# Second attention's scores: one step on four quarters of TensorE's array, instead of two steps on its column halves

## The chip, the cores and the metric

One core of one Trainium2 chip. The metric is the device time of one execution in microseconds (us), lower is better. The kernel before takes 833.54 us, median of 3 runs (831.65 to 834.04).

## The reference

The input is 16 sequences of 512 rows of 128 numbers, f32. Cut to what matters:

```python
x = layernorm(x + attn(x))       # 16 heads of 8, softcap 50 by tanh, causal softmax over 512 rows
x = layernorm(x + ffn(x))        # below, for each of the 16 sequences

weights = x @ router_w + router_b            # a router picks the 63 best rows of 512
sel_idx = sort(top_k(weights, 64).indices[:63])
hn = rmsnorm(x[sel_idx], ln1)
q, kk, v = rope(heads(hn @ wq)), rope(heads(hn @ wk)), heads(hn @ wv)   # 16 heads of 8
sc = einsum('bhqd,bhkd->bhqk', q, kk) / sqrt(8) + m_sel                 # 63 x 63 for each head
a = softmax(sc)
x1 = x[sel_idx] + (a @ v) @ wo
x2 = x1 + gelu(rmsnorm(x1, ln2) @ w1) @ w2
out = zeros.at[sel_idx].set(x2 * weights[sel_idx]) + x * (1 - sel_mask)
```

The change is in `sc`, the scores of this second attention, over the selected rows.

## The kernel before, in words

**Units of work.** The first attention goes batch by batch (16), the routed part goes pair by pair (8 pairs of batches, "q" in the code): the 64 slots of one batch of a pair lie on partitions 0 to 63, those of the other on 64 to 127. The work is cut into steps in six tracks: `prep` (transposes, the query/key and value projections of a batch), `fin` (end of the first attention: divide, output projection, layernorm), `route`, `sel` (gather the selected rows, project them, rotate), `att` (second attention and the first half of the MLP) and `late`. The core of the first attention stands outside the tracks: TensorE's `scores` (L1182, five banks, two units for each group of two heads), ScalarE's tanh (L716) and exp (L731), GpSimd's causal mask (L627), TensorE's `pv` (L1199).

**The order.** An iteration `p` has 16 slots with two halves each. In every half TensorE issues one scores unit and then what `PE_ORDER` lists for that half; ScalarE, GpSimd and VectorE go through their own loops with `ACT_ORDER`, `POOL_ORDER` and `VE_ORDER`. All is written out by hand in these tables, each engine runs its list strictly in order, and waits on semaphores that count the steps of a track. "att.S0@-2" in iteration p is the step for pair p-2, "prep.qk0/1@0" is for the second batch of pair p. GpSimd widens the keys (`att_kw`) in the slot before its last mask of a pair.

**Banks.** Besides the five banks of scores and the one of `pv`, all steps share two PSUM banks, "a" (`ps_a`) and "m" (`ps_m`). `BANK` says which one a step writes, and `BANK_READ` which readers on VectorE TensorE waits for before it writes there.

**The steps of this text.** The keys of a pair (`qkT[:, 1]`, 128 rows of head x 8 + d, 64 slots of each batch) are widened by GpSimd to `k_wide`: for each batch 16 copies, one per head, each multiplied by a mask `head_of` that leaves only that head's 8 rows (L629, called from `att_kw`, two products of 128x1024). A product of the queries (128 rows x 64 slots) with 8 of the 16 copies (512 columns) then gives the scores of 8 heads on 64 partitions, those of one batch. So S0 (`att_scores(q, 0)`, L1356, bank m) is two such products for heads 0 to 7, batch 0 on the left 64 columns of the array and batch 1 on the right; S1 is the same for heads 8 to 15, into bank m again, and waits until VectorE has read S0. Each product in f32 leaves two records in the trace. VectorE reads with `sc` (L1036, scale and add the mask `msel`), then `mx` (L1042, maximum) and `pm` (L1043, subtract), first for S0 and then for S1, with `sc` and `mx` in the same buffers both times. ScalarE's exp of `pm` (L698) follows, and the transposes P0, P1 of the probabilities, copied into `PT` (L1055), which lies in `k_wide`'s memory.

Around them on TensorE: `prep.qk0/1` (L1230, here "qk0"), half of the query/key projection of a batch, bank a; `pv.4/1` and `pv.5/1` (L1199), which start the second half of a batch's heads and wait for GpSimd's masks; `route.thr/1` (L1281), one transpose. On VectorE: `msel` (L1028), and `fin.y0/1` (L877, L879, `y_tm`), which reads bank a. On GpSimd: the masks (two rows of L627 for each group of two heads), and `z_base` (L629).

## Time and profile before

| | |
|---|---|
| Time, median of 3 runs | 833.54 us (831.65 to 834.04) |
| The profiled execution: span from its first to its last instruction | 830.0 us |
| The profiled execution: its own time | the page gives the span alone |
| Busy: TensorE, VectorE, ScalarE, GpSimd | 678.9, 595.4, 554.2, 392.0 us |
| Mean granted TensorE clock | 0.828 of full speed |
| Two L1356 steps of all pairs | 19.1 us busy, 64 records, 675 ns each |
| k_wide products | 30.1 us busy, 16 of them, 1902 ns each |

The page names for each group of instructions its line, its engine, what it writes and reads, and the mean time of one. Busy time is no measure of what a group costs: that depends on whether somebody waits behind it. Records of TensorE overlap, so of a step the time from its first record to the next step's first is what it takes of the engine (here "slot"), some 0.07 us less than to its last record's end. The granted clock is 1.00 at 2.4 GHz and 0.50 at 1.2 GHz.

### The profile page before, as it was taken

What the parts mean: (1) busy time and instruction counts of PE and PEld (TensorE: products, weight loads), DVE (VectorE), ACT (ScalarE), POOL (GpSimd) and SP (SyncE); (2) the same over time, 40 slices, a digit from 0 to 9 for tenths busy, and PEclk for the clock granted to TensorE, in tenths of its full rate; (3) what the DMA queues carried; (4) which work ended last, traced back from release to release, by engine and by line L of the source; (5) the groups of instructions that cost most, each with busy time, mean ns of one, the idle gap of its engine ahead of it and who ended that gap; (6) DMA issues with size and microseconds to landing.
All of it is one profiled execution on the core that took longest, in us unless ns stands there. A gap on an engine that the chain in (4) does not pass through costs nothing.

```text
span 830.0 us, 16995 instructions
## 1 busy us (share of the span) xinstructions
PE 678.9 (82%) x6576; PEld 401.4 (48%) x6576; DVE 595.4 (72%) x1681; ACT 554.2 (67%) x403; POOL 392.0 (47%) x399
## 2 busy tenths in 40 slices
PE   3588787889979988999899988998899879865652
PEld 2344334455546455645455545645565535434232
DVE  4442718777787788958888788769896986588455
ACT  0588688889768876959768876788687968600000
POOL 5263436447544574346455664446546543421201
PEclk8567678899789987989789987899799979985755
DMA  6321302033300503030304030120303030000001
GB/s 190 64 42 37 64 13 53 25 61 119 64 14 17 112 12 67 27 64 14 64 14 90 14 64 15 50 54 2 64 26 65 2 64 27 13 1 26 0 0 51
DMA packets 96913, 36.75 MB, mean 44 GB/s; under 512 B 68018, under 2 KB 94146, under 8 KB 96834
## 3 DMA queue, kind: packets, MB, share of 16 engines
q1 hardware_dynamic: 96834, 35.67, 18.8%
q8 instruction: 53, 0.87, 0.4%
q14 instruction: 26, 0.21, 0.1%
HBM read 14.69 MB, written 4.19 MB: 23 GB/s over the span
## 4 chain that ended last, share of the span: by engine, by line
PE 61%; DVE 18%; issue 10%; ACT 7%; POOL 3%; DMA 1%; POOLq 0%; DVEq 0%; ACTq 0%
PE ps_y L1199 16%; PE ps_s L1182 14%; ACT pr L731 4%; PE ps_m L1308 3%; PE ps_m L1230 3%; ACT th L716 3%; PE ps_m L1206 3%; PE ps_a L1230 3%; PE ps_m L1356 2%; PE ps_a L1393 2%; DVE v_aug L844 2%; PE ps_m L1258 2%; PE ps_a L1206 2%; PE ps_a L1258 1%; PE ps_a L1292 1%
## 5 line engine op out<-in xcount | busy, mean ns | idle before, releaser
L716 ACT ACTIVATE th<-ps_s 128x1024 f32<-128x1024 f32 (+1 forms) x256 | 280.2, 1129 | 110.7 <-PE ps_s L1182 102.0
L627 POOL TENSOR_TENSOR pr<-pr,tri 128x320 f32<-128x320 f32 (+1 forms) x256 | 194.8, 784 | 186.7 <-ACT pr L731 186.7
L731 ACT ACTIVATE pr<-th 128x2304 f32<-128x2304 f32 x128 | 271.5, 2122 | 15.5 <-PE ps_y L1199 15.4
L1182 PE MATMUL ps_s<-q_st,k_st 32*64 32x512 f16 (+7 forms) x2048 | 193.1, 319 | 24.9 <-ACT th L716 20.8
L1199 PE MATMUL ps_y<-pr,v_aug 128*32 128x512 f32 (+7 forms) x2048 | 157.4, 439 | 0.4 <-POOL pr L627 0.4
L1182 PEld LDWEIGHTS ps_s<-q_st,k_st 32*64 32x64 f16 x2048 | 92.3, 114 | 120.0 <-issue 54.3
L1199 PEld LDWEIGHTS ps_y<-pr,v_aug 128*32 128x32 f32 x2048 | 57.0, 113 | 66.9 <-issue 47.4
L641 POOL TENSOR_TENSOR st<-qk,st 128x1024 f16<-128x1024 f32 x32 | 73.8, 2327 | 32.3 <-DVE st L860 32.3
L629 POOL TENSOR_TENSOR k_wide<-qkT,head_of 128x1024 f32<-128x1024 f32 x16 | 30.1, 1902 | 58.0 <-DVE qkT L1029 58.0
L629 POOL TENSOR_TENSOR r<-x,rw_row 128x512 f32<-128x512 f32 x16 | 18.9, 1180 | 63.6 <-DVE x L922 63.6
L702 ACT ACTIVATE hq<-hu 128x512 f32<-128x512 f32 x8 | 5.0, 630 | 60.7 <-POOL hu L629 60.7
L629 POOL TENSOR_TENSOR st<-qk 128x1024 f32<-128x1024 f32 x16 | 30.3, 1892 | 20.0 <-DVE qk L833 19.9
L946 DVE SCALAR_TENSOR_TENSOR wins<-w_wide,x,later 128x512 f16<-128x512 f32 (+1 forms) x64 | 37.8, 590 | 2.5
L698 ACT ACTIVATE pm<-pm 128x1008 f32<-128x1008 f32 x8 | 8.3, 1038 | 42.8 <-DVE pm L1043 42.8
L629 POOL TENSOR_TENSOR z_base<-x,coef 128x512 f32<-128x512 f32 x16 | 18.2, 1136 | 36.9 <-DVE coef L970 36.9
L1308 PE MATMUL ps_m<-mask_a,E 128*64 128x512 f32 x112 | 30.3, 619 | 0.0
L870 DVE COPY y_u<-ps_y 128x512 f32<-128x512 f32 x32 | 21.7, 679 | 8.2 <-PE ps_y L1199 8.1
L844 DVE COPY v_aug<-ps_m 64x512 f32<-64x512 f32 x32 | 22.0, 689 | 7.3 <-PE ps_m L1238 6.8
L1230 PE MATMUL ps_m<-wT,xT 128*128 128x256 f32 x64 | 25.5, 537 | 0.9 <-DVE xT L828 0.9
L1230 PE MATMUL ps_a<-wT,xT 128*128 128x256 f32 x64 | 25.4, 538 | 0.8 <-DVE rank L953 0.8
L1387 PE MATMUL ps_a<-ident,hn 128*128 128x128 f32 x8 | 3.2, 396 | 26.3 <-DVE hn L1082 26.3
L833 DVE COPY qk<-ps_m 128x512 f32<-128x512 f32 x16 | 11.0, 688 | 18.0 <-PE ps_m L1230 18.0
(220 smaller groups left out, 1133.9 us busy)
## 6 DMA issues: line engine op xcount, KB each, us to landing
x_in<-in_L_attn_x SPq DMA_DIRECT2D x16, 256.0 KB, 2.8
x_res<-in_L_attn_x SPq DMA_DIRECT2D x16, 256.0 KB, 3.1
result<-y_out SPq DMA_DIRECT2D x16, 256.0 KB, 2.4
mask_a<-in_L_ffn_attention_mask SPq DMA_DIRECT2D x3, 1024.0 KB, 5.2
pr<-in_L_ffn_attention_mask SPq DMA_DIRECT2D x2, 1024.0 KB, 8.6
w_sb<-in_L_ffn_w SPq DMA_DIRECT2D x2, 256.0 KB
q_st<-st SPq DMA_TRANSPOSE x16, 4.5
k_st<-st SPq DMA_TRANSPOSE x16, 4.7
```

The costliest lines, as they stand in the source:

```text
L627: return nc.gpsimd.tensor_tensor(buf, buf, tri[:, None, :].to_broadcast([P, blocks, 64]), ALU.mult)
L629: mul = lambda out, a, b: nc.gpsimd.tensor_tensor(out, a, b, ALU.mult)
L641: pl["prep"].done(nc.gpsimd.tensor_tensor(lo_parts[s], qk_twice[s], hi_parts[s], ALU.subtract), f"lo_{part}", b)
L716: nc.scalar.activation(th[:, gi % 2, c0:c1], ps_s[:, c0:c1], ACT.Tanh, scale=1.0 / (QK_SCALE ** 2 * DH ** 0.5 * SOFTCAP))\
L731: nc.scalar.activation(pr[:, probs_at(n):probs_at(n) + GROUP], th[:, gi % 2, :], ACT.Exp, scale=SOFTCAP).then_inc(exp_done, 1)
L844: ve["prep"].done(nc.vector.tensor_copy(v_aug[rows, k].rearrange("p b n c -> p (b n) c")[:, :, 16 * s:16 * s + DH], at("prep.v", b)[rows, ...
L946: step(lambda: nc.vector.scalar_tensor_tensor(won[c], w_wide[:, P * c:], x1[:, k, c, D:D + 1], later[:, 0:n], ALU.is_le, ALU.mult, accum_o ...
L1182: last = mm(ps_s[64 * s:64 * s + 64, COL[kb]:COL[kb] + S - 64 * kb], k_st[rows, k, gi // 2, 64 * kb:64 * kb + 64], q_st[rows, k, gi // 2, ...
L1199: last = mm(ps_y[32 * j:32 * j + 32, 64 * kb:S], v_aug[:, k, kb, gi, :], pr[:, c:c + S - 64 * kb], start=(kb == 0), stop=(kb == NB - 1), s ...
L1206: last = tr(bank[:, P * c:P * c + P], src(c), ident[:, :])
L1230: last = mm(at(f"prep.qk{i}", b)[:, :].rearrange("p (n t e) -> p n t e", t=2, e=32)[:, :, t % 2], xT[:, P * t:P * t + P], wT[:, 0:2, :].re ...
L1308: last = mm(at("sel.R")[SLOTS * k:SLOTS * k + SLOTS, :], E[:, c, SLOTS * k:SLOTS * k + SLOTS], (mask_b if k and q < 2 else mask_a)[:, c, : ...
```

## The change

- S0 and S1 become one step S, into both banks. The array is cut in four: heads 0 to 7 live on rows 0 to 63 of queries and keys, heads 8 to 15 on rows 64 to 127, so the product for heads 0 to 7 contracts over the upper 64 rows and writes bank m, the other contracts over the lower 64 and writes bank a; batches on the column halves as before. Four products of 64 rows x 64 columns and 512 columns of moving data instead of four of 128 rows x 64 columns.
- The keys need 8 copies instead of 16, since head h and head h + 8 lie on different rows: the mask `head_in` is the sum of the two halves of `head_of`, made once in the setup, and a k_wide product has 128x512 elements instead of 128x1024. `PT` now covers the k_wide of both batches.
- qk0, which stood between S0 and S1, moves behind the next scores unit, ahead of pv.5. It waits for VectorE's second `sc` (bank a) now; S waits for `y_tm` (bank a) besides `msel` (bank m) and the k_wide products. The threshold's transpose waits for the first `sc`, not the second.
- The scratch memory set aside for DMAs from GpSimd is 4096 bytes.

```diff
-    ["fin.y0T/1@-1"], ["att.S0@-2", "prep.qk0/1@0", "att.S1@-2", "pv.4/1@-1"],
-    ["pv.5/1@-1", "route.thr/1@-2"], ["pv.6/1@-1", "pv.7/1@-1"],
+    ["fin.y0T/1@-1"], ["att.S@-2", "pv.4/1@-1"],
+    ["prep.qk0/1@0", "pv.5/1@-1", "route.thr/1@-2"], ["pv.6/1@-1", "pv.7/1@-1"],
...
     "att.S0": "m",
-    "att.S1": "m",
+    "att.S1": "a",
...
-    "att.P0": ["fin.y0/1@1", "prep.qk0/1@2", "sel.qkT@0"],
+    "att.P0": ["att.sc1@0", "fin.y0/1@1", "prep.qk0/1@2", "sel.qkT@0"],
...
-    "att.S1": ["att.sc0@0"],
+    "att.S1": ["fin.y0/1@1", "prep.xT/1@2", "sel.qkT@0"],
...
-    "prep.qk0/1": ["fin.y0/1@-1", "prep.xT/1@0"],
+    "prep.qk0/1": ["att.sc1@-2", "fin.y0/1@-1", "prep.xT/1@0"],
...
-    "route.thr/1": ["att.sc1@0"],
+    "route.thr/1": ["att.sc0@0"],
...
-        k_wide = sb("k_wide", [P, 2, H, SLOTS])
+        k_wide = sb("k_wide", [P, 2, H // 2, SLOTS])
...
-        PT = k_wide[:, 0].rearrange("p h s -> p (h s)").rearrange("p (n c) -> p n c", n=H // 2)
+        PT = k_wide[:, :, :, :].rearrange("p k h s -> p (k h s)").rearrange("p (n c) -> p n c", n=H // 2)
...
+            pool.wait_ge(const_ready, 19)
+            nc.gpsimd.tensor_tensor(head_in[:, :], head_of[:, 0:H // 2], head_of[:, H // 2:], ALU.add).then_inc(head_in_ready, 1)
...
                     pl["att"].done(mul(
-                        k_wide[:, k], qkT[:, 1, None, SLOTS * k:SLOTS * k + SLOTS].to_broadcast([P, H, SLOTS]),
-                        head_of[:, :, None].to_broadcast([P, H, SLOTS])), f"kw{k}", q)
+                        k_wide[:, k], qkT[:, 1, None, SLOTS * k:SLOTS * k + SLOTS].to_broadcast([P, H // 2, SLOTS]),
+                        head_in[:, :, None].to_broadcast([P, H // 2, SLOTS])), f"kw{k}", q)
...
-            def att_scores(q, h):
+            def att_scores(q, _):
                 pl["att"].wait(t_, q, "kw1")
-                bank_free(f"att.S{h}", q)
+                bank_free("att.S0", q)
+                bank_free("att.S1", q)
                 for k in range(2):
-                    rows = slice(SLOTS * k, SLOTS * k + SLOTS)
-                    last = mm(at(f"att.S{h}")[rows, :], qkT[:, 0, rows],
-                              k_wide[:, k, 8 * h:8 * h + 8, :].rearrange("p h s -> p (h s)"), start=True, stop=True)
-                pe["att"].done(last, f"S{h}", q)
+                    for h in range(2):
+                        last = mm(at(f"att.S{h}")[SLOTS * k:SLOTS * k + SLOTS, :],
+                                  qkT[64 * h:64 * h + 64, 0, SLOTS * k:SLOTS * k + SLOTS],
+                                  k_wide[64 * h:64 * h + 64, k].rearrange("p h s -> p (h s)"), start=True, stop=True)
+                pe["att"].done(last, "S", q)
...
-    nc = _bacc.Bacc("TRN2", target_bir_lowering=False, num_devices=1)
+    nc = _bacc.Bacc("TRN2", target_bir_lowering=False, num_devices=1, dynamic_dma_scratch_size=4096)
```

Names of semaphores in the following rows: `ve_att0` counts VectorE's steps of the second attention, `ve_fin1` those of `fin` for the second batch, `pool_att0` GpSimd's, `masked` the masks, `tanh_done` ScalarE's tanh.

TensorE before, where the scores of a pair are made (first of the pairs, first half of the iteration's first slot):

```order
L1356 MATMUL ps_m<-k_wide,qkT 64x512 [waits ve_sel0,pool_att0]
L1356 MATMUL ps_m<-k_wide,qkT 64x512
L1230 MATMUL ps_a<-wT,xT 128x8x32 [waits ve_prep1,ve_fin1]
L1230 MATMUL ps_a<-wT,xT 128x8x32
L1356 MATMUL ps_m<-k_wide,qkT 64x512 [waits ve_att0,pool_att0]
L1356 MATMUL ps_m<-k_wide,qkT 64x512
L1199 MATMUL ps_y<-pr,v_aug 32x512 [waits ve_fin1,masked]
L1199 MATMUL ps_y<-pr,v_aug 32x512 x3
L1182 MATMUL ps_s<-q_st,k_st 64x512 [waits tanh_done]
```

S0, qk0, S1, pv.4 and the next scores unit, which goes on with three more sizes; behind it come pv.5 and the threshold's transpose. TensorE with the change, same place:

```order
L1363 MATMUL ps_m<-k_wide,qkT 64x512 [waits ve_prep1,ve_fin1,ve_sel0,pool_att0]
L1363 MATMUL ps_a<-k_wide,qkT 64x512
L1363 MATMUL ps_m<-k_wide,qkT 64x512
L1363 MATMUL ps_a<-k_wide,qkT 64x512
L1205 MATMUL ps_y<-pr,v_aug 32x512 [waits ve_fin1,masked]
L1205 MATMUL ps_y<-pr,v_aug 32x512 x3
L1188 MATMUL ps_s<-q_st,k_st 64x512 [waits tanh_done]
L1188 MATMUL ps_s<-q_st,k_st 64x512
L1188 MATMUL ps_s<-q_st,k_st 64x448 x2
L1188 MATMUL ps_s<-q_st,k_st 64x64 x2
L1236 MATMUL ps_a<-wT,xT 128x8x32 [waits ve_fin1,ve_prep1,ve_att0]
L1236 MATMUL ps_a<-wT,xT 128x8x32
```

The wait on `ve_fin1` came to S from qk0, the wait on `ve_att0` to qk0 from S1; qk0 stands behind the scores unit. VectorE with the change, where it reads the scores; before, the same rows with `ps_m` in both:

```order
L1042 SCALAR_TENSOR_TENSOR sc<-ps_m,msel 128x512 [waits ve_sel0,pe_att0]
L1048 TENSOR_REDUCE mx<-sc 128x8 [waits ve_att0]
L1049 TENSOR_TENSOR pm<-sc,mx 128x8x63 [waits ve_att0]
L1042 SCALAR_TENSOR_TENSOR sc<-ps_a,msel 128x512 [waits ve_att0,ve_sel0,pe_att0]
L1048 TENSOR_REDUCE mx<-sc 128x8 [waits ve_att0]
```

VectorE's order did not move; bank a comes free three operations after bank m.

## Rows read from the trace of the kernel before

**Rows 1.** The page, chain of waits that ended last: shares of the span

```profile
PE 61%; DVE 18%; issue 10%; ACT 7%; POOL 3%; DMA 1%; POOLq 0%; DVEq 0%; ACTq 0%
```

**Rows 2.** Busy time by stretch: from:to, length, engines with counts, clock, DMA

```profile
422.20:483.60 61.40, 57.57 (x656) 34.38 (x652) 50.11 (x131) 51.49 (x38) 33.96 (x33) 1.00 0.16 36
```

**Rows 3.** Timeline of TensorE, pair 3: start us, us, engine, instructions, count

```profile
463.43 1.08 PE L1356 MATMUL ps_m<-k_wide,qkT 128*64 128x512 f32 x4
464.44 1.13 PE L1230 MATMUL ps_a<-wT,xT 128*128 128x256 f32 x4
465.50 1.08 PE L1356 MATMUL ps_m<-k_wide,qkT 128*64 128x512 f32 x4
466.51 1.06 PE L1199 MATMUL ps_y<-pr,v_aug 128*32 128x512 f32 x8
467.50 0.62 PE L1182 MATMUL ps_s<-q_st,k_st 32*64 32x512 f16 x6
468.05 0.96 PE L1199 MATMUL ps_y<-pr,v_aug 128*32 128x448 f32 x8
...
469.20 0.73 PE L1182 MATMUL ps_s<-q_st,k_st 32*64 32x384 f16 x10
```

**Rows 4.** Timeline of VectorE, pair 3

```profile
463.27 0.43 DVE L879 TENSOR_TENSOR y_tm<-ps_a,rd 128x256 f32<-128x256 f32 x1
464.56 0.69 DVE L1036 SCALAR_TENSOR_TENSOR sc<-ps_m,msel 128x512 f32<-128x512 f32 x1 [0.86 <-PE ps_m L1356]
...
466.00 1.24 DVE L1043 TENSOR_TENSOR pm<-sc,mx 128x504 f32<-128x504 f32 x1
467.37 0.69 DVE L1036 SCALAR_TENSOR_TENSOR sc<-ps_m,msel 128x512 f32<-128x512 f32 x1
...
468.81 0.68 DVE L1043 TENSOR_TENSOR pm<-sc,mx 128x504 f32<-128x504 f32 x1
```

**Rows 5.** Timelines of GpSimd and ScalarE, pair 3

```profile
459.19 3.76 POOL L629 TENSOR_TENSOR k_wide<-qkT,head_of 128x1024 f32<-128x1024 f32 x2 [5.33 <-DVE qkT L1029]
462.91 2.79 POOL L627 TENSOR_TENSOR pr<-pr,tri 128x320 f32<-128x320 f32 x4
465.65 1.05 POOL L629 TENSOR_TENSOR z_base<-x,coef 128x512 f32<-128x512 f32 x1
...
461.40 2.12 ACT L731 ACTIVATE pr<-th 128x2304 f32<-128x2304 f32 x1
...
469.97 1.24 ACT L716 ACTIVATE th<-ps_s 128x1280 f32<-128x1280 f32 x1 [0.78 <-PE ps_s L1182]
```

**Rows 6.** Timeline of GpSimd, pair 0 (its S0 starts at 194.27)

```profile
196.85 1.57 POOL L629 TENSOR_TENSOR z_base<-x,coef 128x512 f32<-128x512 f32 x1
```

**Rows 7.** Timelines of TensorE and GpSimd where qk0 moves without any S

```profile
114.57 2.07 PE L1230 MATMUL ps_a<-wT,xT 128*128 128x256 f32 x4
...
118.44 0.62 PE L1182 MATMUL ps_s<-q_st,k_st 32*64 32x512 f16 x6
...
114.50 1.41 POOL L627 TENSOR_TENSOR pr<-pr,tri 128x320 f32<-128x320 f32 x2 [2.85 <-ACT pr L731]
```

**Rows 8.** Timelines of TensorE and VectorE, pairs 6 and 7

```profile
724.68 1.08 PE L1356 MATMUL ps_m<-k_wide,qkT 128*64 128x512 f32 x4 [1.03 <-POOL k_wide L629]
...
784.72 1.97 PE L1356 MATMUL ps_m<-k_wide,qkT 128*64 128x512 f32 x4 [1.64 <-POOL k_wide L629]
...
783.12 0.22 DVE L1028 COPY msel<-ps_m 128x64 f32<-128x64 f32 x1 [1.12 <-PE ps_m L1340]
...
789.59 0.69 DVE L1036 SCALAR_TENSOR_TENSOR sc<-ps_m,msel 128x512 f32<-128x512 f32 x1 [0.73 <-PE ps_m L1356]
```

**Rows 9.** Busy time of a stretch as rows 2; timeline of TensorE, pairs 4 and 5

```profile
391.50:401.70 10.20, 10.20 (x58) 7.59 (x62) 9.79 (x29) 7.52 (x6) 5.05 (x4) 0.50 0.01 2
...
554.46 1.08 PE L1356 MATMUL ps_m<-k_wide,qkT 128*64 128x512 f32 x4
...
640.86 1.08 PE L1356 MATMUL ps_m<-k_wide,qkT 128*64 128x512 f32 x4
```

More of the change, by code:

```diff
@@ L92 @@
     "sel": ["gather", "ET", "hnT", "qkv", "R", "qkT", "RT", "msel"],
-    "att": ["S0", "S1", "P0T", "P1T", "PV", "oT", "wo", "h2T", "w1"],
+    "att": ["S", "P0T", "P1T", "PV", "oT", "wo", "h2T", "w1"],
     "late": ["w2", "sc0", "sc1"],
@@ L334, in build @@
         head_of = sb("head_of", [P, H])
+        head_in = sb("head_in", [P, H // 2])
         half_of = sb("half_of", [P, 2, DH])
@@ L467, in build @@
         gate_ready = sem("gate_ready")
+        head_in_ready = sem("head_in_ready")
         turned = [sem(f"turned{i}") for i in range(2)]
@@ L658, in att_kw @@
                 pe["att"].wait(pool, q - 1, "PV")
+                if q == 0:
+                    pool.wait_ge(head_in_ready, 1)
                 for k in range(2):
                     pl["att"].done(mul(
-                        k_wide[:, k], qkT[:, 1, None, SLOTS * k:SLOTS * k + SLOTS].to_broadcast([P, H, SLOTS]),
-                        head_of[:, :, None].to_broadcast([P, H, SLOTS])), f"kw{k}", q)
+                        k_wide[:, k], qkT[:, 1, None, SLOTS * k:SLOTS * k + SLOTS].to_broadcast([P, H // 2, SLOTS]),
+                        head_in[:, :, None].to_broadcast([P, H // 2, SLOTS])), f"kw{k}", q)
             def att_hh(q, _):
@@ L1033, in att_scores @@
                 step = chain(ve["att"], q)
-                pe["att"].wait(v, q, f"S{h}")
+                pe["att"].wait(v, q, "S")
                 ve["sel"].wait(v, q, "msel")
@@ L1417, in _ @@
                      "sel.ET": sel_ET, **{f"sel.R{c or ''}": (lambda q, _, c=c: sel_R(q, c)) for c in range(NT)}, "sel.RT": sel_RT, "sel.hnT": sel_hnT, "sel.qkv": sel_qkv,
-                     "sel.msel": sel_msel, "sel.qkT": sel_qkT, "att.S0": lambda q, _: att_scores(q, 0),
-                     "att.S1": lambda q, _: att_scores(q, 1), "att.P0": lambda q, _: att_P(q, 0),
+                     "sel.msel": sel_msel, "sel.qkT": sel_qkT, "att.S": att_scores,
+                     "att.P0": lambda q, _: att_P(q, 0),
                      "att.P1": lambda q, _: att_P(q, 1), "att.PV": att_PV, "att.oT": att_oT, "att.wo": att_wo,
```

## Prediction, made before the changed kernel ran

> **What bounds the kernel now.** I read the chain of waits first: 61% of the span lies on TensorE and 18% on VectorE [rows 1]. Then the busy time by stretch: over the 61.4 us that hold one whole set of the changed steps TensorE is busy for 57.57 us at a granted clock of 1.00, ScalarE for 51.49, VectorE for 50.11, GpSimd for 33.96 [rows 2]. So TensorE sets the pace, in program order, and a microsecond saved or lost on it counts unless it stands waiting nearby. Work taken from GpSimd counts only where somebody waits for it. Last I read the timelines around the changed steps, one engine at a time [rows 3 to 5]. What lies there does so for each of the pairs 0 to 5, the same to 0.1 us in TensorE's rows; pairs 6 and 7 come when the first attention has nothing left to issue.
>
> **The steps as they are.** From 463.43: S0 (to 464.44), the keys-and-queries projection qk0 (to 465.50), S1 (to 466.51), pv.4 (to 467.50), a scores unit (to 468.05), pv.5 and the threshold's transpose, and the next scores unit at 469.20 [rows 3]. Nothing waits in this stretch: S1 waits by program for VectorE's first `sc`, which starts at 464.56 and takes 0.69 [rows 4], but qk0 fills that time. That is what the old order is good for. The whole is 5.77 us.
>
> **Part by part.**
>
> *S0 and S1 become one step S.* S0 is two products of 512 columns on the two column halves, together, and ends after 1.08 us. S is four, on four quarters of the array. No row shows two products on different rows and the same columns. Lower bound: all four run together as the two do now, 1.08. Upper bound: the two row halves run one after the other, one more slot of S0 (463.43 to 464.44, 1.01), 2.09. The near relatives speak for the lower one, since both column halves, and in pv four column quarters (1.06 for the same 512 columns), cost one product's time [rows 3]. I take 1.08. The Trainium skill, "TensorEngine Tiling (Array Packing)", sections Key Properties and Gotcha 1, says that tiles operate independently and that row tiles only have to write different banks, as S does; that gives the lower bound too, and no row of this trace shows it.
>
> *S now needs two banks.* S0 needed only bank m, free since the `msel` copy. Bank a is free when VectorE has read it for `y_tm`: 463.27 + 0.43 = 463.70 [rows 4]. TensorE is there at 463.43. So S starts at 463.75: a wait of 0.3 us that qk0 used to have covered, since it came one step later. S ends at 464.83.
>
> *pv.4 follows S directly.* It waits for GpSimd's masks. Exp ends at 461.40 + 2.12 = 463.52, two masks take 2.79 / 2 = 1.4, so they are done at 464.95 at best, against 465.70 today, when the two k_wide products (3.76) stand ahead of them [rows 5]. The products now have 512 elements each, as z_base has in 1.05, so some 1.7 us less: GpSimd is no longer the late one. pv.4 starts at 465.0, and with slots of 0.99 and 0.55 TensorE is past the scores unit at 466.55.
>
> *qk0 has moved behind the scores unit, and waits for the second `sc`.* It writes bank a, which now holds the second half of S. VectorE reads it only after `sc`, `mx`, `pm` of the first half. From S's end: 0.05 to the first `sc`, 1.44 to `pm`, `pm` 0.68, 0.13 to the second `sc`, and that 0.69 [rows 4], 2.99 in all, so 467.82. TensorE came at 466.55 and stands for 1.3 us; behind qk0 stand pv.5, the threshold and the next scores unit, for which ScalarE already waited 0.78 [rows 5]. qk0 runs from 467.87 to 468.93, pv.5 and the threshold take 1.15, and the scores unit starts at 470.08 instead of 469.20: **0.88 us later, not 1.0 earlier**. Six pairs: +5.3.
>
> *Where `pm` and z_base meet.* In pair 3 `pm` took 1.24 rather than 0.68 because z_base ran from 465.65 [rows 4, 5]; with GpSimd earlier and `pm` at 466.3 they miss each other, and the 0.68 above stands. In pairs 0 and 1 exp ends later, z_base starts at 196.85 [rows 6], and the new `pm` would start at 197.16, inside it. The rows price a meeting at 0.56. Two pairs: +1.1. The Trainium skill, "SBUF — State Buffer", section "SBUF: two separate sides", has a lock for this: whichever of a GpSimd operation and a VectorE operation with two SBUF inputs starts first blocks the other for its whole length. By that rule these two pairs lose 0.7 each, 1.5 in all, and the trace agrees (1.24 is what is left of z_base from 466.00, 0.70, and `pm`'s 0.54).
>
> *The first projection that moves without any S (batch 1 of pair 1).* pv.4 now comes to its masks at 114.57 and they end at 114.50 + 1.41 = 115.91; so far qk0 covered that [rows 7]. The wait is 1.4. qk0 behind it may run at the full clock then, 1.13 instead of 2.07, or not: +0.4 to +1.4. I take 0.5, since the scores unit next to its new place takes the 0.62 of the full clock.
>
> *The end.* Pair 7 lies on the chain. There S0 waits for the products until 784.72, takes 1.97, and the second `sc` starts at 789.59. Now GpSimd is done 1.7 earlier, S waits for `msel` (783.12 + 0.22), starts at 783.40, ends at 785.37, the first `sc` comes at 785.42, and the second 1.44 + 0.68 + 0.13 later, at 787.67 [rows 4, 8]. -1.9. In pair 6 S0 waited 1.03 for the products [rows 8]: at best that much is gained, at worst the 0.3 of the wait for `y_tm` is lost, and VectorE goes on from there in its own order; I take 0.
>
> *The rest.* `head_in` is one small GpSimd operation in the setup, long before the first pair needs it; VectorE's instructions are the same but for the bank that they read; the smaller scratch for DMAs from GpSimd has no user, since all DMAs go from SyncE. 0 each; nobody waits for them, so there is no cover that could go.
>
> *The clock.* Two new waits, 0.3 and 1.3 us, stand within 4.5 us. The stretch of rows 2 kept 2.4 GHz with single waits of about one us; 391.5 to 401.7 ran at 1.2 GHz, all busy, after a stretch with several waits [rows 9]. Such a stretch costs half its length, 5.1 us. I take no net change, with 9 us less and 10 us more as bounds (rivals 3 and 4).
>
> **Sum.** 5.3 + 1.1 + 0.5 - 1.9 = +5.0. The profiled execution has a span of 830.0 and the page gives nothing else of its time; the median of the runs is 833.54, 3.5 above. So a span of 835.0, and **838.5 us**.
>
> **The rivals.**
> 1. *The sum holds* (0.45): 838.5, between 834 and 843 as the first projection, the meetings and some of the clock go.
> 2. *The change doesn't do what it says: the row halves don't overlap* (0.18). Then S lasts 1.0 longer, all of it ahead of the waits for `sc`: six times 1.0, 1.0 in pair 6, 1.97 in pair 7 at half clock, +9.0: 847.5. For it: no row shows the contrary. Against it: columns do overlap.
> 3. *The clock falls after the new waits* (0.12), in two of the six pairs, 5.1 each: +10.2, 848.7. For it: the waits are longer than any around these steps today. Against it: S and pv stand between them.
> 4. *Faster: the clock's slow stretches come to lie better* (0.13). S0 of pairs 4 and 5 start 91.03 and 86.40 after the one before [rows 3, 9], with the same instructions; the difference is clock alone. Every later step moves by tenths of a us, and where a slow stretch starts may change. If two of the long pairs become like the short one, that is -9.2 + 5.0, -4.2: 829.3. It decides from a saving of 5.0, a little more than one such pair.
> 5. *The delay isn't passed on* (0.12). If ScalarE or VectorE set the pace behind these steps, the 6.4 us vanish in TensorE's other waits, and the end's 1.9 remains: 832.1, or 835 with half of it. Against it: ScalarE's wait of 0.78 for just this scores unit, and TensorE's 94% busy.
>
> **How the numbers follow.** A measurement of this kernel tells 0.3% or 2.5 us from no change, so "the same" is 831.0 to 836.0. Faster: rival 4, 0.13. Same: rival 5 and 0.10 of the first case, 0.22. Slower: the rest, 0.65. The range from 830.5 to 849.0 leaves out most of rival 4 and the upper ends of 2 and 3, 0.2 together.
>
> **What would show it.** In the profile after: k_wide products near 1.05; S as one group of eight records of about 1.1 (2.1 if rival 2); TensorE idle some 1.3 before qk0 with VectorE's `sc` as the releaser, in six places; that group in the list of waits with 7 to 9 us; S released by `y_tm`; at the end the second `sc` 1.9 earlier against the end of the span. No such wait before qk0, or pv.5 earlier than today against S, would prove the argument wrong; a sum of busy time and waits that agrees while the total doesn't would point to the clock.

## The result, and the profile after

The changed kernel takes **837.69 us**, median of 6 runs (835.27 to 840.08); the kernel before, run beside it, 833.85 us (831.65 to 834.04). The ratio is 1.0055, with an interval of 1.0034 to 1.0075: slower by 3.8 us, where 5.0 more was forecast (838.5 against 833.54). A ratio, here and below, is taken over the runs within 1.5% of the fastest of the same kernel, with a 95% interval; a median is over all runs.

The page of the changed kernel: span, busy times, the chain by engine, and two groups (line, engine, operation, count, busy us, mean ns, idle before and what ended it).

```profile
span 833.2 us, 17003 instructions
...
PE 672.0 (81%) x6576; PEld 401.2 (48%) x6576; DVE 596.9 (72%) x1681; ACT 554.8 (67%) x403; POOL 377.7 (45%) x400
...
PE 57%; DVE 20%; issue 9%; ACT 8%; POOL 5%; DMA 1%; POOLq 0%; DVEq 0%; ACTq 0%
...
L1236 PE MATMUL ps_a<-wT,xT 128*128 128x256 f32 x64 | 24.9, 529 | 8.2 <-issue 7.3
...
L633 POOL TENSOR_TENSOR k_wide<-qkT,head_in 128x512 f32<-128x512 f32 x16 | 16.4, 1044 | 57.2 <-DVE qkT L1035 57.2
```

GpSimd has 14 us less to do and TensorE 7 us less, and the kernel is slower: of the chain, 61% lay on TensorE [rows 1], now 57%, with more on VectorE and GpSimd. The qk0 group has the new wait, 7.3 us of it in six places. The page calls its releaser "issue", which names nobody; the timeline does. TensorE, pair 3 (start us, duration, engine, line, what, count, idle before):

```profile
459.89 0.61 PE L1363 MATMUL ps_m<-k_wide,qkT 64*64 64x512 f32 x1 [0.41 <-issue]
459.90 0.64 PE L1363 MATMUL ps_a<-k_wide,qkT 64*64 64x512 f32 x1
...
460.39 0.59 PE L1363 MATMUL ps_a<-k_wide,qkT 64*64 64x512 f32 x1
461.04 1.07 PE L1205 MATMUL ps_y<-pr,v_aug 128*32 128x512 f32 x8
462.03 0.62 PE L1188 MATMUL ps_s<-q_st,k_st 32*64 32x512 f16 x6
464.08 1.10 PE L1236 MATMUL ps_a<-wT,xT 128*128 128x256 f32 x4 [1.43 <-issue]
...
466.26 0.73 PE L1188 MATMUL ps_s<-q_st,k_st 32*64 32x384 f16 x10
```

VectorE and ScalarE beside it:

```profile
459.25 0.42 DVE L885 TENSOR_TENSOR y_tm<-ps_a,rd 128x256 f32<-128x256 f32 x1
461.04 0.69 DVE L1042 SCALAR_TENSOR_TENSOR sc<-ps_m,msel 128x512 f32<-128x512 f32 x1 [1.36 <-PE ps_a L1363]
461.76 0.68 DVE L1048 TENSOR_REDUCE mx<-sc 128x8 f32<-128x504 f32 x1
462.48 0.68 DVE L1049 TENSOR_TENSOR pm<-sc,mx 128x504 f32<-128x504 f32 x1
463.29 0.69 DVE L1042 SCALAR_TENSOR_TENSOR sc<-ps_a,msel 128x512 f32<-128x512 f32 x1
...
467.03 1.24 ACT L722 ACTIVATE th<-ps_s 128x1280 f32<-128x1280 f32 x1 [2.16 <-PE ps_s L1188]
```

S is eight records in 1.09 us (459.89 to 460.39 + 0.59): all four quarters of the array run at once, which ends the rival of row halves one after the other (2.09). The second `sc` ends at 463.98 and qk0 starts at 464.08. A step that waits for nothing starts 0.07 us ahead of the end of the record before it, so S is due at 459.89 - 0.41 - 0.07 = 459.41. From there to the next scores unit it is 6.85 us, where the old order took 5.77 [rows 3]: 1.08 lost; ScalarE waits 2.16 us for that unit instead of 0.78 [rows 5].

The other place is the rest of the pair. Below, TensorE where the next named step starts, pair 3 of the changed kernel, and then of the kernel before:

```profile
481.77 2.04 PE L1264 MATMUL ps_m<-wT,yT 128*128 128x128 f32 x8 [0.64 <-DVE yT L894]
496.22 0.33 PE L1395 MATMUL ps_a<-ident,hn 128*128 128x128 f32 x1 [3.30 <-DVE hn L1088]
518.99 1.13 PE L1408 MATMUL ps_m<-w_sb,hu 128*128 128x128 f32 x8 [1.20 <-DVE v_aug L850]
```

```profile
484.71 2.05 PE L1258 MATMUL ps_m<-wT,yT 128*128 128x128 f32 x8 [1.17 <-DVE yT L888]
499.56 0.33 PE L1387 MATMUL ps_a<-ident,hn 128*128 128x128 f32 x1 [3.30 <-DVE hn L1082]
522.32 0.91 PE L1400 MATMUL ps_m<-w_sb,hu 128*128 128x128 f32 x6 [1.06 <-DVE v_aug L844]
```

Counted from where S or S0 is due (459.41 and 463.43), the output projection `fin.wo` starts after 22.36 against 21.28 us, `h2T` (the transpose of `hn`) after 36.81 against 36.13, `w2` after 59.58 against 58.89. The whole 1.08 is still there at `fin.wo`, though its wait is 0.53 shorter: that went to a scores unit ahead of it that now runs at 1.2 GHz (1.70 us instead of 1.17). Behind it less of the same slow stretch is left, and 0.4 is found again by `h2T`; 0.7 stays. In these two pairs the clock ran at 1.2 GHz in nearly the same places, so they can be compared; most pairs can't, and that is the rest of the story.

### The profile page after: what moved, and what is told of

The parts are those of the page before. It is cut to its first block, busy times and chain, and to the rows that moved or that the text cites. A ratio compares the mean times of both kernels' runs of the same rounds, so it can differ in the third digit from the quotient of the medians.

```text
span 833.2 us, 17003 instructions
## 1 busy us (share of the span) xinstructions
PE 672.0 (81%) x6576; PEld 401.2 (48%) x6576; DVE 596.9 (72%) x1681; ACT 554.8 (67%) x403; POOL 377.7 (45%) x400
## 4 chain that ended last, share of the span: by engine, by line
PE 57%; DVE 20%; issue 9%; ACT 8%; POOL 5%; DMA 1%; POOLq 0%; DVEq 0%; ACTq 0%
PE ps_y L1205 16%; PE ps_s L1188 12%; ACT pr L737 5%; PE ps_m L1314 3%; ACT th L722 3%; PE ps_m L1236 3%; PE ps_m L1212 3%; PE ps_a L1236 3%; POOL pr L631 2%; PE ps_a L1401 2%; DVE v_aug L850 2%; PE ps_m L1264 2%; DVE wins L952 2%; PE ps_a L1298 2%; PE ps_a L1264 1%
## 5 line engine op out<-in xcount | busy, mean ns | idle before, releaser
L633 POOL TENSOR_TENSOR k_wide<-qkT,head_in 128x512 f32<-128x512 f32 x16 | 16.4, 1044 | 57.2 <-DVE qkT L1035 57.2
L1236 PEld LDWEIGHTS ps_a<-wT,xT 128*128 128x128 f32 x64 | 16.2, 266 | 14.2 <-issue 11.6
```

What stands on the lines that cost most here:

```text
L633: mul = lambda out, a, b: nc.gpsimd.tensor_tensor(out, a, b, ALU.mult)
L1236: last = mm(at(f"prep.qk{i}", b)[:, :].rearrange("p (n t e) -> p n t e", t=2, e=32)[:, :, t % 2], xT[:, P * t:P * t + P], wT[:, 0:2, :].re ...
```

## The experiments

Twelve kernels, in four groups, each on one chip (1 to 4, 5 to 8, 9 to 11, and 12); the kernel before ran beside each group at 832.4, 833.8, 832.1 and 833.2 us. Each kernel has one profile, so what follows pair by pair is of one execution. Pairs 0 to 5 are counted from the start of S (or S0) in pair 0 to its start in pair 6. "Half clock" is time at a granted clock of 0.50 (1.2 GHz).

**1. The narrow keys alone** (two steps, S0 on the upper rows, S1 on the lower, qk0 between them).

```diff
...
-                    last = mm(at(f"att.S{h}")[rows, :], qkT[:, 0, rows],
-                              k_wide[:, k, 8 * h:8 * h + 8, :].rearrange("p h s -> p (h s)"), start=True, stop=True)
+                    last = mm(at(f"att.S{h}")[rows, :], qkT[64 * h:64 * h + 64, 0, rows],
+                              k_wide[64 * h:64 * h + 64, k].rearrange("p h s -> p (h s)"), start=True, stop=True)
```

> The kernel before with the keys widened to 8 heads, S0 on the upper 64 rows and S1 on the lower 64, still two steps into bank m with qk0 between them. Theory (the loss of the change is the exposed wait for VectorE's second sc, the narrower keys pay only at the end): pairs 0 to 5 as in the kernel before, the k_wide products 1.7 us shorter in sum, pair 7's second sc 1.3 to 1.7 us earlier, so 832.2 us. Rival (the products on 64 rows are dearer by themselves, by draining or by the clock): S0 and S1 longer than 1.08 us, or TensorE's time per pair longer than before, 835 us or more.

836.21 us (ratio 1.0028, interval 0.9996 to 1.0061; 829.39 to 841.63 but for one run at 912). Not the 832.2 expected, and not told from no change. The order at the scores is that of before, and so is the path: from S0 to the next scores unit it is 5.76 us in all of the pairs 0 to 5, against 5.77. S0 and S1 on 64 rows take 1.08 us as on 128, which ends the rival that such products are dearer. The end is shorter: from pair 6 to the last instruction 103.9 us, against 105.3. Yet pairs 0 to 5 take 535.6 us against 530.4, with the same steps in the same order on TensorE; 133.1 us of them are at half clock, against 119.5. Pair 0, where the half-clock stretches lie in the same places, takes 88.05 us against 88.04; the 5 us lie in the pairs where they don't.

**2. qk0 behind the next scores unit, 3. both `sc` ahead of `mx`, 4. qk0 directly behind S.** Each is the changed kernel with one edit: in 2 qk0 comes half a slot later, when the second `sc` is done; in 3 `sc` gets a second buffer, and VectorE frees bank a before it goes on; in 4 qk0 waits the full time.

```diff
-    ["prep.qk0/1@0", "pv.5/1@-1", "route.thr/1@-2"], ["pv.6/1@-1", "pv.7/1@-1"],
+    ["pv.5/1@-1", "route.thr/1@-2"], ["prep.qk0/1@0", "pv.6/1@-1", "pv.7/1@-1"],
...
-    "att": ["sc0", "mx0", "sub0", "sc1", "mx1", "sub1", "den", "rden", "PT0", "PT1", "o0", "o1", "oT", "x1f",
+    "att": ["sc0", "sc1", "mx0", "sub0", "mx1", "sub1", "den", "rden", "PT0", "PT1", "o0", "o1", "oT", "x1f",
...
-    ["fin.y0T/1@-1"], ["att.S@-2", "pv.4/1@-1"],
-    ["prep.qk0/1@0", "pv.5/1@-1", "route.thr/1@-2"], ["pv.6/1@-1", "pv.7/1@-1"],
+    ["fin.y0T/1@-1"], ["att.S@-2", "prep.qk0/1@0", "pv.4/1@-1"],
+    ["pv.5/1@-1", "route.thr/1@-2"], ["pv.6/1@-1", "pv.7/1@-1"],
```

> The changed kernel with qk0 one half slot later, behind the second scores unit and ahead of pv.6. Theory (the wait of qk0 for the second sc costs what it lasts, 1.43 us in pairs 2 to 5 and 0.79 in pairs 0 and 1): the second sc ends before TensorE comes to qk0, no wait there, pv.6 starts 1.4 us earlier in pairs 2 to 5, the scores unit 2.5 us earlier; 7.3 us less than the changed kernel, 830.4 us. Rival (the move of qk0 itself is what costs, since VectorE and later steps want it early): no better than 837.7, or worse. Rival clock: mean granted clock well off 0.82 to 0.83, time off the sum by more than 3 us.

> The changed kernel with VectorE reading both banks first (sc, sc, mx, pm, mx, pm, with a second sc buffer); TensorE's order untouched. Theory: the second sc ends 1.5 us after S instead of 3.0, pv.4 and the scores unit cover it, qk0 doesn't wait; next scores unit 1.4 us earlier in pairs 2 to 5, 0.8 in pairs 0 and 1, so 7.3 us less than the changed kernel, 830.4 us. Rival (row order or clock): no gain beyond 2 us.

> The changed kernel with qk0 directly behind S, ahead of pv.4, so that pv.4 and a scores unit stand behind the wait instead of covering it. Theory: the wait grows from 1.4 to 3.1 us, the second scores unit comes 1.6 us later in each of pairs 0 to 5, 9.5 us more than the changed kernel, 847 us. Rival (the wait is idle time that costs nothing): within 2 us of 837.7.

845.46 us (ratio 1.0158, interval 1.0121 to 1.0194), 845.82 (1.0166, 1.0125 to 1.0207) and 859.41 (1.0316, 1.029 to 1.0342). The first two were expected at 830.4 and miss by 15 us, to the other side; the fourth was expected at 847 and misses by 12. At the place itself the first two did what they should. TensorE in the second, pair 3 (S starts at 472.39), and in the third (S at 472.94):

```profile
475.97 0.32 PE L1287 MATMUL ps_m<-ident,edge 128*128 128x128 f32 x1
476.22 0.73 PE L1188 MATMUL ps_s<-q_st,k_st 32*64 32x384 f16 x10
476.88 1.13 PE L1236 MATMUL ps_a<-wT,xT 128*128 128x256 f32 x4
...
493.44 2.05 PE L1264 MATMUL ps_m<-wT,yT 128*128 128x128 f32 x8 [1.76 <-DVE yT L894]
```

```profile
475.70 1.10 PE L1236 MATMUL ps_a<-wT,xT 128*128 128x256 f32 x4
...
477.87 0.73 PE L1188 MATMUL ps_s<-q_st,k_st 32*64 32x384 f16 x10
...
493.39 1.92 PE L1264 MATMUL ps_m<-wT,yT 128*128 128x128 f32 x8 [1.17 <-DVE yT L894]
```

Nothing waits before qk0, and the scores unit (in the second ahead of qk0, in the third behind it) comes 3.83 and 4.93 us behind S's start instead of 6.37. In the second most of this is gone at `fin.wo`, which waits 1.76 us for `yT` instead of 0.64 and so starts 21.05 us behind S instead of 21.88; in the third it starts at 20.45. So the wait before qk0 is real, taking it away gains 0.8 to 1.4 us as far as `fin.wo`, and still the kernels are slower by 8. In the fourth the wait does more than last. Pair 3 (S at 475.56):

```profile
479.75 2.04 PE L1236 MATMUL ps_a<-wT,xT 128*128 128x256 f32 x4 [3.11 <-issue]
481.73 1.94 PE L1205 MATMUL ps_y<-pr,v_aug 128*32 128x512 f32 x8
```

The wait of qk0 is 3.11 us (3.5 in pairs 0 and 1), and behind it qk0 and pv.4 run at half clock: 2.04 and 1.94 us instead of 1.10 and 1.07. A half-clock stretch of 6.8 us begins here, 2.2 to 3.6 us behind S's start, in each of the pairs 0 to 5. The second scores unit comes 3.9 us later than in the change, not 1.6: 1.7 of it is the longer wait, 2.2 the clock. From S to `h2T` it is 39.5 to 41.0 us in pairs 0 to 4, against 35.0 to 36.4 in the change, so this delay does pass on. It is the forecast's third rival, the clock falling at the new wait: in the change, at 1.4 us, it didn't come; here, at 3.1, it comes in all six pairs.

Where the 8 us went shows when each pair is cut at `w2`'s start. The stretch from `w2` to the next pair's S, in the view of busy time by stretch (from:to, length, PE, PEld, DVE, ACT, POOL busy with counts, clock, DMA): the changed kernel, pairs 3 and 4; before, pairs 2 and 3; the second experiment, pairs 2 and 3; the third, pairs 2 and 3.

```profile
519.00:548.50 29.50, 28.05 (x289) 17.53 (x290) 22.78 (x71) 24.58 (x19) 15.12 (x16) 1.00 0.39 72
607.80:640.20 32.40, 30.98 (x289) 19.18 (x290) 22.41 (x71) 24.43 (x18) 14.98 (x16) 0.89 0.28 58
```

```profile
434.40:463.40 29.00, 27.86 (x285) 17.42 (x285) 22.54 (x71) 24.17 (x18) 15.60 (x14) 1.00 0.33 74
522.30:554.50 32.20, 31.14 (x287) 19.30 (x287) 22.31 (x71) 24.20 (x18) 15.63 (x14) 0.89 0.30 66
```

```profile
438.20:472.40 34.20, 32.67 (x287) 19.41 (x288) 22.55 (x71) 24.69 (x19) 15.12 (x16) 0.85 0.29 63
531.00:563.60 32.60, 31.14 (x287) 19.32 (x287) 22.52 (x71) 24.52 (x18) 15.07 (x16) 0.90 0.30 66
```

```profile
435.70:472.90 37.20, 36.80 (x285) 23.68 (x285) 24.06 (x71) 22.39 (x17) 13.98 (x15) 0.73 0.26 57
529.40:559.00 29.60, 28.19 (x285) 17.46 (x285) 22.96 (x71) 24.93 (x19) 15.22 (x17) 1.00 0.36 72
```

The same work, in 285 to 289 records of TensorE, takes 29.0 to 29.6 us at a clock of 1.00, 32 to 34 at 0.90 to 0.85, and 37.2 at 0.73, whichever kernel it is. Of the pairs 0 to 4, two have such a late stretch at half clock in the profile of before, one in that of the change, four in the second experiment; in the third two have one, of 20.5 and 6.8 us. Over pairs 0 to 5 these last parts sum to 189.4 and 188.9 us in the second and third experiments, against 178.6 in the change: 10.9 and 10.3 us more, where the six pairs as a whole take 10.4 more in both. So the 8 us lie there. Not all of it need be the clock: in pair 4 of the third, whose last part takes 34.4 us with 6.8 at half clock, TensorE also waits 2.71 us ahead of `sc1`. What I expected of these kernels had no term for the clock, and it is larger than the terms they had.

**5. The change with the keys widened to sixteen heads again.**

> The change with the keys widened to sixteen heads again (two products of 1.90 us instead of 1.04 us); the scores stay one step on 64 rows each. Theory (local prices): in pairs 0 to 5 the products end well before S is due, so nothing there; in pairs 6 and 7 S comes 0.9 to 1.7 us later each: 837.7 + 2.5 = 840.2 us (839 to 842). Rival (the narrower products cost in the middle, because z_base and pm now meet there in pairs 0 and 1): 837 us or less. Rival (the time is set by where the 1.2 GHz stretches fall, any edit moves them): anywhere from 833 to 846, with the difference to the change's own profile in the stretches from 20 and from 68 us behind S, not at S.

837.66 us (ratio 1.0026, interval 0.9986 to 1.0066; 830.48 to 841.78), not the 840.2 expected. The narrower products (1.04 us instead of 1.90) can't be told from the wide ones in the time; in the profiles the end has some of it, 107.3 us from pair 6 on against 105.9 in the change. This kernel's profile is of its fastest run, and pair by pair it is a twin of the change's: S starts 86.3, 88.0, 88.4, 88.6 us apart for pairs 0 to 4, against 86.3, 87.9, 88.5, 88.6. Then come 88.7 and 84.2 against 91.7 and 87.1, for in the change 6.8 and 10.2 us more of these two pairs run at half clock. Of the 5.0 us between the two spans (828.1 and 833.2) those two pairs hold 5.9. Pair 4 here, the last stretch cut as above, is to be held against 607.80 of the change:

```profile
607.20:636.60 29.40, 27.99 (x285) 17.46 (x286) 22.73 (x71) 24.48 (x19) 15.99 (x15) 1.00 0.29 64
```

**6 to 8. Filling TensorE's waits, to hold the clock.** Ahead of `h2T` TensorE idles for 3.3 us, and behind it pairs 1 to 4 have 10.2 us at half clock, pair 0 has 6.8. Five products of 256 columns that nobody reads go into the bank of `h2T` there; once in the change, once in the kernel before. In the eighth the products of `sc0` are computed twice besides.

```diff
-                ve["att"].wait(t_, q, "hn2")
                 bank_free("att.h2T", q)
+                for _i in range(5):
+                    mm(at("att.h2T")[:, 0:2 * P], wT[:, 3, :], wT[:, 0:2, :].rearrange("p a d -> p (a d)"), start=True, stop=True)
+                ve["att"].wait(t_, q, "hn2")
```

> The change plus five products of 256 columns written into the bank of h2T before TensorE waits for hn, where it sits idle 3.3 to 3.8 us in every pair; nothing reads them. Theory A (the granted clock decides: the idle 3.3 us is what brings the 10.3 us at 1.2 GHz that begin right behind it in each pair, and half of the difference between kernels is where such stretches fall): the stretch from 36 to 47 us behind S goes, each such stretch costs some 3 to 4 us in a pair, so about 837.7 - 6 x 3.3 = 818 us (808 to 828). Theory B (the clock falls whatever TensorE does there, or the chain over VectorE bounds): 837 to 845 us, the fillers only cost.

> The kernel before with the same five products. Theory A: the same gain as in the change, 833.9 - 20 = 814 us (804 to 824); and since with the clock held what is left between the two kernels is their own path, the change with the fillers should be slower than this one by the 5 to 8 us that six pairs times 1.1 to 1.5 us at the scores minus 2.7 us at the end make. Theory B: 833 to 841 us.

> The change with the fillers and with the products of sc0 computed twice (1.16 us more of work in the place where TensorE otherwise waits 1.0 us for the bank of sc1). Theory A: the stretch from 68 us behind S, which in the change's profile is in one pair of four and cost 3 us there, goes in all pairs; 1 to 4 us less than the kernel with the fillers alone. Theory B (VectorE's step behind sc0 is on the path): 3 to 6 us more than with the fillers alone.

843.54 us (ratio 1.0118, interval 1.0077 to 1.0158), 851.26 (836.27 to 851.91 and one far above, too scattered for a ratio) and 847.59 (1.0182, 1.0122 to 1.0242), where Theory A had 818, 814 and less than the sixth. It falls as I had put it: not one gained, and even the fastest run of the seventh is slower than the kernel before. The sixth in pair 3:

```profile
502.55 2.42 PE L1395 MATMUL ps_a<-wT 128*128 128x256 f32 x10 [0.29 <-DVE x1f L1079]
505.02 0.33 PE L1397 MATMUL ps_a<-ident,hn 128*128 128x128 f32 x1
505.28 1.17 PE L1188 MATMUL ps_s<-q_st,k_st 32*64 32x512 f16 x16
...
508.31 1.95 PE L1403 MATMUL ps_a<-h2T,w_sb 128*128 128x128 f32 x8 [1.28 <-DVE h2T L1091]
```

The filler did keep the clock: the scores unit behind `h2T` takes 1.17 us where it took 1.68 in the change. But the step behind it then waits 1.28 us for VectorE (0.30 in the change) and starts 3.29 us behind `h2T` in both kernels, so what the clock gave went into a wait. The slow stretch comes all the same, from 40 us behind S instead of 37, and in two pairs at 47 and again at 71. In sum the sixth has 16 us less at half clock than the change (271 against 287) and is 6 us slower; where it loses them no run separates. At this place 1.2 GHz was nearly free; it costs where TensorE is the bound. The eighth missed its aim: in three of the pairs 0 to 4 TensorE still waits 0.9 us ahead of `sc1` and has a late stretch, of 3.4 us.

**9 to 11. The wait ahead of `sc1`, made longer.** 67 us behind S, where the late stretches begin, TensorE waits 1.0 us for `yT` (bank of `sc1`). I moved the first `pv` unit up in between; in the change, in the kernel before, and in the second experiment's kernel.

```diff
-    [], ["fin.yT/0@0", "late.sc0@-2", "late.sc1@-2", "fin.wo/0@0", "pv.0/1@0"],
+    [], ["fin.yT/0@0", "late.sc0@-2", "pv.0/1@0", "late.sc1@-2", "fin.wo/0@0"],
```

> The change with one unit of second products of the first attention (8 records, 1.07 us) moved up between sc0 and sc1, where TensorE waits 0.8 to 1.0 us for the bank. Theory C (in the profiles so far a pair that has a third stretch at 1.2 GHz, beginning 67 to 71 us behind S at that wait, takes 3 us more than one without; how many pairs have one makes most of the difference between these kernels): with the wait gone no pair has it, 0.6 us of waiting goes too: 837.7 - (1 to 2) x 3 - 6 x 0.6 = 830 us (827 to 833), and the runs lie closer together than the 5 to 11 us seen so far. Rival (the third stretch comes from elsewhere or costs nothing): 834 to 838 us.

> The kernel before with the same move. Theory C: its profile had the third stretch in two pairs of four, so 833.9 - 6 - 3.6 = 824 us (821 to 829), and what stays between this kernel and the change with the same move is the path by the scores, 1.1 us in each pair at the start, of which 0.2 to 0.5 us was left at h2T: the change slower by 1 to 6 us. Rival: 830 to 834 us.

> The kernel with qk0 moved behind the next scores unit (it took 845.5 us, with a third stretch in all four middle pairs of its profile), with the same move. Theory C: the third stretches go, 845.5 - 4 x 3 - 3.6 = 830 us (826 to 834), level with or 1 to 3 us under the change with the move, since no wait stands ahead of qk0 there. Rival (qk0 being late costs by another way): over 838 us.

864.47 us (852.78 to 868.99; ratio 1.0272, interval 1.0194 to 1.035), 865.57 (846.31 to 867.24 and one far above; 1.0221, 1.012 to 1.0322) and 873.65 (856.16 to 884.47; 1.0336, 1.0247 to 1.0425), where 830, 824 and 830 were expected. The profiled executions took 867.8, 865.4 and 881.4 us; their totals aren't compared, their pairs can be. The edit missed its aim: pv isn't ready there, its masks come later. From the ninth, pairs 3 and 4 (TensorE, then the stretches as above):

```profile
551.07 1.07 PE L1205 MATMUL ps_y<-pr,v_aug 128*32 128x512 f32 x8 [1.71 <-POOL pr L631]
639.80 1.94 PE L1205 MATMUL ps_y<-pr,v_aug 128*32 128x512 f32 x8 [1.55 <-POOL pr L631]
```

```profile
541.40:571.50 30.10, 27.97 (x285) 17.41 (x286) 22.48 (x71) 24.49 (x19) 15.02 (x16) 1.00 0.42 71
629.90:666.10 36.20, 34.08 (x285) 20.07 (x286) 22.91 (x71) 25.11 (x19) 15.25 (x17) 0.81 0.25 52
```

The waiting there has grown from 1.0 us to between 1.15 and 1.8 in eleven of the fifteen pairs; and the late stretch at half clock is now there in 3, 4 and 5 of the pairs 0 to 4, in eleven of these twelve for 10 us and more. Two of the twelve, the longest (23.9 and 27.3 us), begin already at `w2`, 61 us behind S, as the 20.5 us of the third experiment do. Where it is absent (pair 3) the last part takes 30.1 us, 0.6 more than in the change; where it follows (pair 4) 36.2. So in one kernel, behind the same wait, it comes or doesn't, and that makes 6 us. The two waits (1.71 without, 1.55 with) show that it isn't the length alone. That the longer wait is what brought the stretches is likely and not shown, since the edit also put pv ahead of `sc1`.

**12. The same wait taken away, in the kernel before.**

```diff
-    ["prep.ss/0@1", "prep.root1/0@1", "sel.xs@-1"], ["prep.root2/0@1", "prep.qkn/0@1", "fin.yT/0@0", "sel.ss@-1"],
+    ["prep.ss/0@1", "prep.root1/0@1", "sel.xs@-1"], ["prep.root2/0@1", "fin.yT/0@0", "prep.qkn/0@1", "sel.ss@-1"],
```

> The kernel before with two steps of VectorE exchanged: the copy of yT (0.68 us) ahead of the product of q and k with their norms (1.23 us). In the profile of before the copy ends 531.24 us and TensorE waits 1.01 us for it ahead of sc1; now it should end at 530.1, as sc0 ends at 530.3, so the wait goes and no other comes. Theory C (a wait 67 us behind S is what brings the third stretch at 1.2 GHz, 3 us for 6.8 us of it and 6 us for 13.6 us; making that wait longer by 0.6 us brought it to 13.6 us in nearly every pair): without the wait no pair has it; before's profile has it in two pairs of the middle four, so 833.9 - 2 x 3 - 5 x 0.9 = 823 us (820 to 829). Rival (the stretch follows from something else, such as the waits 8 us earlier, and the copy is hidden): 831 to 835 us.

841.64 us (ratio 1.0098, interval 1.0071 to 1.0124), where 823 was expected. Missed again. TensorE, pair 3:

```profile
534.32 1.16 PE L1409 MATMUL ps_a<-x,ET 64*128 64x128 f32 x8
535.22 1.13 PE L1409 MATMUL ps_m<-x,ET 64*128 64x128 f32 x8
537.99 1.13 PE L1258 MATMUL ps_a<-wT,yT 128*128 128x128 f32 x8 [1.64 <-DVE sel_v L808]
```

The wait ahead of `sc1` is gone, and `fin.wo` behind it waits 1.64 us: it writes bank a, where `sc0` lies until VectorE has read it. VectorE does that behind both exchanged steps, as before (it ends at 537.05 + 0.68), so the exchange brought TensorE to `fin.wo` sooner and not VectorE to that read. So it is in four of the pairs 0 to 4; in pair 2 the old wait is still there, 0.86 us. The late stretch comes in pairs 0, 1 and 2, 6.8 us each, and not in 3 and 4. My "no other comes" was the error: I had looked at the one step and not at who waits for VectorE next.

## Why the prediction was right

**The path.** Step by step, for pair 3 unless said:

| Term | forecast | measured |
|---|---|---|
| S, four quarters at once | 1.08 | 1.09 |
| S waits for bank a | 0.3 | 0.41 |
| wait of qk0 for the second `sc` | 1.3 | 1.43 (0.79 in pairs 0, 1) |
| loss up to the next scores unit | 0.88 | 1.08 |
| pairs 0 and 1 besides (`pm` meets z_base) | 0.56 each | 0.42 each |
| first qk0 without any S | 0.5 | 2.9 at the place |
| end, pairs 6 and 7 | -1.9 | +0.7, half clock in it |

S and its overlap are as taken. The Trainium skill, "TensorEngine Tiling (Array Packing)", section Key Properties, says that tiles work independently; this trace agrees, with eight records in 1.09 us on row halves and column halves together. S starts 0.22 us behind the end of `y_tm` (459.25 + 0.42), not the 0.05 I took; it waits on four semaphores. In pair 0 `pm` takes 1.10 us beside z_base:

```profile
199.72 1.10 DVE L1049 TENSOR_TENSOR pm<-sc,mx 128x504 f32<-128x504 f32 x1
...
199.24 1.04 POOL L633 TENSOR_TENSOR z_base<-x,coef 128x512 f32<-128x512 f32 x1
```

What is left of z_base from 199.72 is 0.56, and 0.54 more make the 1.10; before, in pair 3, it was 0.70 and 0.54. That is close to one after the other, as the Trainium skill has it ("SBUF — State Buffer", "SBUF: two separate sides"). Beside the 0.68 of `pm` alone it costs 0.42, and that is what the next scores unit is later than in the other pairs (7.26 us from where S is due, instead of 6.84). pv.4 waits 1.11 us for masks in these two pairs, but that only takes from the wait of qk0.

**What I had sized wrongly.** (a) "+5.3" took all of the 0.88 as passed on. It is 1.08 at the scores, of which 0.7 reaches `w2`, read in pair 3, where the clock lets the two kernels be compared. That is rival 5 in part: not "vanishes", but 0.4 in a pair. Six pairs would make 6 x 0.7 = 4.2, and 0.8 more in pairs 0 and 1 at most. (b) The first qk0 without an S costs 2.9 us and not 0.5. The wait of pv.4 for its masks is 1.32 us (the forecast's 1.4 is 1.34 by its own rows); I had counted on qk0 to run at full clock behind it, and it ran at half, with all its neighbours:

```profile
114.64 1.93 PE L1205 MATMUL ps_y<-pr,v_aug 128*32 128x512 f32 x8 [1.32 <-POOL pr L631]
116.50 1.06 PE L1188 MATMUL ps_s<-q_st,k_st 32*64 32x512 f16 x6
117.49 2.07 PE L1236 MATMUL ps_a<-wT,xT 128*128 128x256 f32 x4
```

The slow stretch lasts to 121.5 us, before to 118.5. At the end of the scores unit ahead of this pv.4 the change had been 1.3 us ahead (113.32 against 114.64, by the clock); at the end of the one ahead of the first S it is 2.4 behind (196.73 against 194.34), and S's own wait makes it 2.87 (197.14 against 194.27). At the place itself, ScalarE's tanh of the scores unit behind pv.4 starts at 117.60 against 119.10 before, that of the next unit at 122.09 against 120.66: 1.5 ahead has become 1.4 behind. In the third, fifth and sixth experiments, with the same order there, the same count gives 2.9, 2.9 and 2.5; in the first and fourth, with the old order there, 0.0. So this loss belongs to the moved step. (c) The end: from the start of S or S0 in pair 6 it is 105.94 us, against 105.27 before, and no gain of 1.9. In pair 7 the gain is there and larger: S waits for `msel`, and from the first k_wide product to the second `sc` it is 5.94 us (786.85 to 792.79), against 8.68 before (780.91 to 789.59), so 2.7 less. The sum had S at half clock there (1.97); the first `sc` starts 1.15 us behind S's start. But between S of pair 6 and S of pair 7 the change took 62.2 us against 60.0, with 44 us at half clock against 31. The first experiment, with the same narrow products and 34 us at half clock there, shows a gain of 1.4 us.

**The clock.** I took "no net change, with 9 us less and 10 us more". In the profiles of the change and of before half clock sums to 287 us in both. That it came out even is luck as much as judgement: it is 7 us more up to the first S, 14 less in pairs 0 to 5, 7 more from pair 6. It did not come out even in the second and third experiments (294 and 318 us), which are better at the disputed place and slower by 8 us. Rival 3, the clock falling behind the two new waits, didn't happen: the wait ahead of qk0 (1.4 us, 0.8 in pairs 0 and 1) is followed by full clock in all six pairs. It wasn't far away: at 3.1 us, in the fourth experiment, it happened in all six, and pair 0 of the ninth, whose order here is that of the change, has 6.8 us at half clock from pv.4 on (1.93 us, behind its wait of 1.11 for masks). Rival 4's mechanism is what the runs showed most of, in both directions. In the fifth experiment it is 5.9 us between two pairs of kernels that are otherwise twins, in the ninth 6 us between two pairs of one kernel.

So the forecast was right in its sign and its mechanism, its largest term short by 0.2 us at the place and over by 0.2 at the end of the pair. In the two profiles the sum closes: 2.87 up to the first S, -0.3 over pairs 0 to 5 (530.4 us before, 530.1 after) and +0.7 from pair 6, together 3.2, the difference of the spans. Term by term that is not the sum forecast: it had 0.5 for the start, 6.4 for pairs 0 to 5 and -1.9 for the end. The start and the end came out 2.4 and 2.6 higher, the pairs 6.7 lower, and that these nearly cancel is luck. The -0.3 is itself a sum: 4.2 to 5.0 of the path, an estimate from (a), and as much back from the clock (105.8 us of these pairs at half clock instead of 119.5), most of it in the late stretches (one that cost 3.0 us, instead of two of 4.7 and 3.1, each against 29.0 to 29.5 without), the rest in both directions.

**Open.** What decides whether a late stretch follows the wait at `sc1`. With a longer wait there it came in most pairs; but with the wait gone and another just behind it, it came in two of four, and equal waits (1.02 and 0.99 us in pairs 3 and 4 of the change) had it once and once not. Pairs 0 and 5 say more than I read from them: in the kernel before, the change and the first eight experiments TensorE waits at most 0.24 us ahead of `sc1` there, and of these 20 pairs one has a late stretch (pair 5 of the fourth), where of the 40 pairs 1 to 4 of the same kernels, nearly all with a wait there of 0.8 us or more, 22 have one. So the wait has to do with it. But these pairs also wait less at `w2`, and no experiment took the waits away in pairs 1 to 4, so that the stretch would vanish then is argued and not shown. No version beat the kernel before.

## What to carry to other kernels

Where two halves are merged into one step on TensorE, look at what used to fill the wait between them: here qk0, between the two halves, hid VectorE's reading of the first, and the merged step with its second bank lost 1.1 us per pair at the scores that no saving on GpSimd could return, since nobody waited for GpSimd there. Price a lost microsecond to the next place where the engine waits anyway, not at its own place; and before moving a step in a hand-written order, list who waits next on the engine that it now delays. Where TensorE's clock falls and rises within each round, compare equal pieces at equal granted clock before explaining a difference of one per cent: a piece of 29 us took up to 37 with the same instructions.

## What the runs showed of the hardware that I had not expected

- Four f32 products on four quarters of the array, two on different rows of the same columns, start within 0.02 us of each other and are through after 1.09 us, where two take 1.08.
- A wait of 3.1 us ahead of a step was followed by 6.8 us at 1.2 GHz in six pairs of six, one of 0.8 to 1.4 us ahead of the same step in none of six (the fourth experiment and the change).
- A wait of 1.0 us, in a stretch where TensorE is otherwise busy all the time (28.05 of 29.50 us), is sometimes followed by 7 to 10 us at 1.2 GHz and sometimes not, in one program from pair to pair (the change and the kernel before). A pair with it takes 3 us more, and with 14 us of it 6 us more.
- Half clock costs less than half its length even where TensorE is busy: 6.8 us of it cost 3.0 (pairs 3 and 4 of the change), 13.6 us cost 6.1 (the ninth). Where the engine goes on to wait for VectorE it costs nearly nothing: filling such a wait kept the clock for the next unit (1.17 us instead of 1.68) and the wait behind it grew by 1.0 us.
